# Cross attention of a decoder layer: row maxima packed on 128 partitions, another order of the steps, and expert weights scaled by ScalarE

## What is computed

```python
def _L0_xattn_ref(query, key, value, ...):          # query 32x112x256, key = value 32x375x256
    q, k, v = query @ qw.T + qb, key @ kw.T + kb, value @ vw.T + vb
    # 16 heads of 16; each head's q and k are cut in two halves of 8
    logits_1 = einsum('bhtd,bhsd->bhts', q1, k1) * SCALING
    logits_2 = einsum('bhtd,bhsd->bhts', q2, k2) * SCALING
    a1, a2 = softmax(logits_1), softmax(logits_2)
    diff_weights = a1 - lam * a2
    attn_output = einsum('bhts,bhsd->bhtd', diff_weights, v) * (1.0 - LAMBDA_INIT)
    return attn_output (heads joined) @ out_proj_weight.T + out_proj_bias
x = _layernorm(x + attn(x)); x = _layernorm(x + xattn(x, ctx, ctx)); x = _layernorm(x + ffn(x))
```

## Time and profile before

| | us |
|---|---|
| median of the runs (3 runs, 1745.75 to 1752.3) | 1746.22 |
| span of the profiled execution | 1765.9 |
| start of the first cross maxima to the last item's projection read | 438.8 to 1174 |
| cross turn without routing work | 21.06 |

### The profile page before, as it was taken

One profiled execution on the slowest core, in us unless ns is written; L12 is line 12 of the kernel. 1 busy time (PEld: TensorE's weight loads), 2 busy tenths in 40 slices (PEclk: granted clock), 3 DMA queues, 4 the chain that ended last, 5 costly groups with the idle time before them and its releaser, 6 DMA issues. The chain is left out here.

```text
span 1765.9 us, 46393 instructions
## 1 busy us (share of the span) xinstructions
PE 1566.4 (89%) x17664; PEld 1193.8 (68%) x17664; DVE 1117.6 (63%) x2617; ACT 897.4 (51%) x2175; POOL 759.0 (43%) x916
## 2 busy tenths in 40 slices
PE   4899999995899998999899989847999999999991
PEld 2577777774466666666566666526888888888891
DVE  5566666664788888878877877643454444444443
ACT  2345544543466666666666656523444444444444
POOL 6334334432675555776577567530111211212212
PEclk9899999998799999999999989868999999999996
DMA  6666666653665555565455445237777777767744
GB/s 179 181 182 185 190 190 187 185 154 77 161 170 150 143 141 138 148 160 144 136 157 158 136 116 162 72 125 274 250 247 245 256 241 246 268 228 252 273 139 176
DMA packets 205509, 318.93 MB, mean 181 GB/s; under 512 B 61000, under 2 KB 174056, under 8 KB 205288
## 3 DMA queue, kind: packets, MB, share of 16 engines
q1 hardware_dynamic: 180648, 248.48, 46.8%
q0 software_dynamic: 21504, 66.19, 12.5%
q10 hardware_dynamic: 3136, 1.30, 0.3%
HBM read 224.52 MB, written 91.03 MB: 179 GB/s over the span
## 5 line engine op out<-in xcount | busy, mean ns | idle before, releaser
L1208 DVE TENSOR_REDUCE cross_mx<-cross_bank_max 112x2 f32<-112x750 f32 x512 | 457.9, 932 | 123.7 <-PE cross_bank_max L1323 120.4
L1021 ACT ACTIVATE cross_probs<-cross_bank_score 125x448 f32<-125x448 f32 x768 | 399.0, 546 | 255.0 <-PE cross_bank_score L1313 220.1
L1323 PE MATMUL cross_bank_max<-ckst,cqst 96*112 96x375 f16 x1024 | 265.2, 342 | 31.1 <-DVE cross_mx L1208 20.4
L1500 POOL DMA_INDIRECT acc<-experts_y,experts_dest_i x64 | 98.7, 1543 | 442.7 <-ACT experts_y L1537 372.4
L1577 DVE TENSOR_TENSOR experts_hid<-experts_bank_h,experts_gated 128x256 f32<-128x256 f32 (+1 forms) x288 | 113.6, 394 | 261.6 <-ACT experts_gated L1526 257.7
L1313 PE MATMUL cross_bank_score<-cqst,ckst 97*125 97x448 f16 x768 | 267.8, 368 | 9.2 <-ACT cross_probs L1021 6.4
L1609 PE MATMUL experts_bank_h<-experts_x_hi,experts_w_more 128*128 128x256 f16 (+1 forms) x1536 | 234.0, 264 | 0.0
L1323 PEld LDWEIGHTS cross_bank_max<-ckst,cqst 96*112 96x112 f16 x1024 | 116.6, 133 | 125.0 <-DVE cross_mx L1208 99.3
L1609 PE MATMUL experts_bank_h<-experts_x_lo,experts_w_more 128*128 128x256 f16 (+1 forms) x768 | 196.2, 264 | 0.0
L1526 ACT ACTIVATE experts_gated<-experts_bank_h 128x256 f32<-128x256 f32 (+1 forms) x288 | 103.7, 360 | 166.9 <-PE experts_bank_h L1609 163.4
L1339 PE MATMUL cross_bank_out<-cross_probs,cross_val 125*32 125x112 f32 x6144 | 181.2, 266 | 1.5 <-issue 1.5
(11 more groups left out here) (241 smaller groups left out, 3045.9 us busy)
## 6 DMA issues: line engine op xcount, KB each, us to landing
experts_w_more<-w_halves SPq DMA_DIRECT2D x24, 3072.0 KB, 12.2
w<-w_halves SPq DMA_DIRECT2D x12, 3072.0 KB, 12.6
cross_ew<-in_experts POOLq DMA_DIRECT2D x32, 768.0 KB
w_halves<-cross_ew_half POOLq DMA_DIRECT2D x32, 768.0 KB, 7.5
ckst<-cross_k SPq DMA_DIRECT2D x96, 187.5 KB
cross_v<-front_v SPq DMA_DIRECT2D x24, 531.2 KB
cross_val<-cross_v SPq DMA_DIRECT2D x32, 398.4 KB
front_src<-in_ctx_t SPq DMA_DIRECT2D x24, 500.0 KB, 8.9
```

What stands on the lines that cost most here:

```text
L1021: nc.scalar.activation(probs[:, e % PROBS], bank_score[e % 2][0:SC, 0:4 * T], ACT.Exp, scale=CROSS_SCALE).then_inc(probs_ready, 1)
L1208: nc.vector.tensor_reduce(mx[:, b % nb, 2 * n:2 * n + 2], bank_max[n % 2][0:T, :, 0:S], AX.X, ALU.max).then_inc(max_read, 1)
L1323: last = nc.tensor.matmul(bank_max[n % 2][0:T, i, 0:S], qst[0:STACK, p, u // 4, (u % 4) * T:(u % 4 + 1) * T], kst[0:STACK, p, u // 4, :], ...
```

## The change

In `cross`:

- The query rows of an item are cut into 28 stripes of 128 rows (`stripe`) in place of 32 units of 112. Fourteen pairs take the place of sixteen, each reduced over 128 partitions. Where a stripe crosses from one group of 4 units (448 rows) to the next, which stripes 3, 10, 17 and 24 do, it is computed by two matmuls of 64 stationary columns each, into partitions 0 to 63 and 64 to 127. The row transposes and their DMAs go by 14 stripes of 128.
- `MAX_AT` and `REDUCE_AT` list the parts of the fourteen pairs in PE's and in DVE's stream. The order of the steps becomes `turn`, `score`, `row1`, `out1`, `heads`, `row0`, `proj`, `out0`, with other parts, and `turn`, `score`, `row1` and `row0` are read in the same part in which they are computed.
- The multiplication of the expert weights by 64 moves from POOL to ACT (`scale_weights`, after the exponentials of parts 13, 14 and 15). `ew` and `ew_half` and their semaphores are doubled, and loads run two cuts ahead.

```diff
-STEP_AT = {"turn": (1, -2), "row1": (4, 0), "score": (6, -2), "out1": (8, -1), "heads": (13, -1),
-           "row0": (15, 1), "proj": (17, -1), "out0": (21, 0)}
-READ_AT = {"turn": (2, -2), "row1": (5, 0), "score": (7, -2), "out1": (9, -1), "heads": (14, -1),
-           "row0": (16, 1), "proj": (18, -1), "out0": (22, 0)}
-EVACUATE_AT = ((14, 0), (2, -1))
-AGGREGATE_AT, NORMALISE_AT = 19, 23
+STEP_AT = {"turn": (2, -2), "score": (4, -2), "row1": (6, 0), "out1": (8, -1), "heads": (11, -1), "row0": (14, 1), "proj": (15, -1), "out0": (17, 0)}
+READ_AT = {"turn": (2, -2), "score": (4, -2), "row1": (6, 0), "out1": (9, -1), "heads": (12, -1), "row0": (14, 1), "proj": (17, -1), "out0": (20, 0)}
+EVACUATE_AT = ((15, 0), (4, -1))
+AGGREGATE_AT, NORMALISE_AT = (18, -1), (23, -1)
...
+SCALE_AT = (13, 14, 15)
...
-def maximum_at(e):
-
-    return SPAN // 3 * 2 * (e // SPAN) + e % SPAN - FIRST_MAX if e % SPAN >= FIRST_MAX else None
+QUERIES = UNITS * T
+LANES = 128
+STRIPES = QUERIES // LANES
+PAIRED = STRIPES // 2
+MAX_AT = (1, 3, 4, 6, 6, 10, 11, 14, 15, 17, 17, 20, 21, 23)
+REDUCE_AT = (0, 1, 1, 3, 7, 10, 12, 13, 17, 18, 19, 19, 20, 23)
+
+
+def at_part(table, e):
+
+    return [n for n, at in enumerate(table) if at == e]
+
+
+def stripe(j):
+
+    lo, hi, wide = LANES * j, LANES * (j + 1), 4 * T
+    cuts = sorted({lo, hi, *(g * wide for g in range(GROUPS) if lo < g * wide < hi)})
+    return [(a // wide, a % wide, a - lo, b - a) for a, b in zip(cuts, cuts[1:])]
...
-        mx = ph.sb("mx", [T, nb, UNITS], F32)
-        neg_mx = ph.sb("neg_mx", [16, nb, 2, T], F16)
+        mx = ph.sb("mx", [LANES, nb, STRIPES], F32)
+        neg_mx = ph.sb("neg_mx", [PAIRED, nb, 2, LANES], F16)
...
-        ew = ph.sb("ew", [128, CUT], F32)
+        ew = ph.sb("ew", [128, 2, CUT], F32)
         ew_big = ph.sb("ew_big", [128, CUT], F32)
-        ew_half = ph.sb("ew_half", [128, 2, CUT], F16)
+        ew_half = ph.sb("ew_half", [128, 2, 2, CUT], F16)
...
-                        wait(sp, ew_stored, 16 * CUTS)
+                        for p in range(2):
+                            wait(sp, ew_stored[p], 16 * CUTS // 2)
...
-                pool.dma_start(ew[:], a["experts"][0]).then_inc(ew_loaded, 16)
+                for b in range(2):
+                    pool.dma_start(ew[:, b], a["experts"][b]).then_inc(ew_loaded[b], 16)
...
                 def split_weights(b, group, ready):
-                    wait(pool, ew_loaded, 16 * (b + 1))
-                    wait(pool, ew_stored, 16 * b)
+                    p = b % 2
+                    wait(pool, ew_stored[p], 16 * (b // 2))
                     for i in range(pieces):
                         cols = slice(i * piece, (i + 1) * piece)
                         n = pieces * b + i + 1
-                        pool.tensor_scalar(ew_big[:, cols], ew[:, cols], WSCALE, None, ALU.mult).then_inc(ew_big_ready, 1)
                         wait(pool, ew_big_ready, n)
-                        if i == pieces - 1 and on(b + 1):
-                            pool.dma_start(ew[:], a["experts"][b + 1]).then_inc(ew_loaded, 16)
-                        pool.tensor_copy(ew_half[:, 0, cols], ew_big[:, cols]).then_inc(ew_hi_ready, 1)
+                        if i == pieces - 1 and on(b + 2):
+                            pool.dma_start(ew[:, p], a["experts"][b + 2]).then_inc(ew_loaded[p], 16)
+                        pool.tensor_copy(ew_half[:, p, 0, cols], ew_big[:, cols]).then_inc(ew_hi_ready, 1)
                         wait(pool, ew_hi_ready, n)
-                        pool.tensor_tensor(ew_half[:, 1, cols], ew_big[:, cols], ew_half[:, 0, cols],
+                        pool.tensor_tensor(ew_half[:, p, 1, cols], ew_big[:, cols], ew_half[:, p, 0, cols],
                                            ALU.subtract).then_inc(ew_ready, 1)
                         scatter(group, ready, i)
                     wait(pool, ew_ready, pieces * (b + 1))
-                    pool.dma_start(w_halves[b], ew_half[:]).then_inc(ew_stored, 16)
+                    pool.dma_start(w_halves[b], ew_half[:, p]).then_inc(ew_stored[p], 16)
...
-                        nc.scalar.activation(neg_mx[:, p, h], bank[0:16, 0:T], ACT.Copy, scale=-1.0).then_inc(read[name], 1)
+                        nc.scalar.activation(neg_mx[:, p, h], bank[0:PAIRED, 0:LANES], ACT.Copy, scale=-1.0).then_inc(read[name], 1)
                         wait(act, read[name], b + 1)
-                        act.dma_start(qst[STACK:STACK + 1, p, 4 * h:4 * h + 4, :].rearrange("o g (i t) -> o (g i) t", t=T),
-                                      neg_mx[:, p, h]).then_inc(row_loaded[h][p], 16)
+                        act.dma_start(qst[STACK:STACK + 1, p, 4 * h:4 * h + 4, :].rearrange("o g n -> o (g n)").rearrange(
+                            "o (j n) -> o j n", n=LANES), neg_mx[:, p, h]).then_inc(row_loaded[h][p], 16)
...
+                def scale_weights(b, i):
+                    cols = slice(i * piece, (i + 1) * piece)
+                    wait(act, ew_loaded[b % 2], 16 * (b // 2 + 1))
+                    wait(act, ew_ready, pieces * (b - 1) + i + 1)
+                    nc.scalar.activation(ew_big[:, cols], ew[:, b % 2, cols], ACT.Copy, scale=WSCALE).then_inc(ew_big_ready, 1)
...
+                        for i in at_part(SCALE_AT, e) if on(c + 2) else ():
+                            scale_weights(c + 2, i)
...
-                        if e == AGGREGATE_AT and on(c - 1):
-                            wait(dve, stats_ready, c)
                         if (c, e) in (LAMBDA_AT[0], LAMBDA_AT[2]):
                             difference(LAMBDA_AT.index((c, e)))
-                        n = maximum_at(e)
-                        if n is not None and on(c + lead):
+                        for n in at_part(REDUCE_AT, e) if on(c + lead) else ():
                             b = c + lead
-                            wait(dve, max_full, 2 * GROUPS * b + n + 1)
-                            nc.vector.tensor_reduce(mx[:, b % nb, 2 * n:2 * n + 2], bank_max[n % 2][0:T, :, 0:S],
+                            wait(dve, max_full, PAIRED * b + n + 1)
+                            nc.vector.tensor_reduce(mx[:, b % nb, 2 * n:2 * n + 2], bank_max[n % 2][:, :, 0:S],
                                                     AX.X, ALU.max).then_inc(max_read, 1)
-                        if e == AGGREGATE_AT and on(c - 1):
-                            p = (c - 1) % nb
+                        if e == AGGREGATE_AT[0] and on(c + AGGREGATE_AT[1]):
+                            b = c + AGGREGATE_AT[1]
+                            p = b % nb
+                            wait(dve, stats_ready, b + 1)
                             nc.vector.bn_aggr(mv[:, p], stats[:, p]).then_inc(mv_ready, 1)
...
-                    wait(pe, max_read, 2 * GROUPS * b + n - 1)
+                    wait(pe, max_read, PAIRED * b + n - 1)
                     for i in range(2):
-                        u = 2 * n + i
-                        last = nc.tensor.matmul(bank_max[n % 2][0:T, i, 0:S], qst[0:STACK, p, u // 4, (u % 4) * T:(u % 4 + 1) * T],
-                                                kst[0:STACK, p, u // 4, :], start=True, stop=True)
+                        for g, col, lane, size in stripe(2 * n + i):
+                            last = nc.tensor.matmul(bank_max[n % 2][lane:lane + size, i, 0:S], qst[0:STACK, p, g, col:col + size],
+                                                    kst[0:STACK, p, g, :], start=True, stop=True)
...
-                        wait(pe, max_read, 2 * GROUPS * b + GROUPS * (h + 1))
-                        last = nc.tensor.transpose(bank[0:16, 0:T], mx[:, p, 16 * h:16 * h + 16], ident[0:T, 0:T])
+                        wait(pe, max_read, PAIRED * b + PAIRED // 2 * (h + 1))
+                        last = nc.tensor.transpose(bank[0:PAIRED, 0:LANES], mx[:, p, PAIRED * h:PAIRED * (h + 1)], ident[:])
...
-                        n = maximum_at(e)
-                        if n is not None and on(c + lead):
+                        for n in at_part(REDUCE_AT, e) if on(c + lead) else ():
                             b = c + lead
-                            wait(dve, max_full, 2 * GROUPS * b + n + 1)
-                            nc.vector.tensor_reduce(mx[:, b % nb, 2 * n:2 * n + 2], bank_max[n % 2][0:T, :, 0:S],
+                            wait(dve, max_full, PAIRED * b + n + 1)
+                            nc.vector.tensor_reduce(mx[:, b % nb, 2 * n:2 * n + 2], bank_max[n % 2][:, :, 0:S],
                                                     AX.X, ALU.max).then_inc(max_read, 1)
-                        if e == AGGREGATE_AT and on(c - 1):
-                            p = (c - 1) % nb
+                        if e == AGGREGATE_AT[0] and on(c + AGGREGATE_AT[1]):
+                            b = c + AGGREGATE_AT[1]
+                            p = b % nb
+                            wait(dve, stats_ready, b + 1)
                             nc.vector.bn_aggr(mv[:, p], stats[:, p]).then_inc(mv_ready, 1)
```

(21 more changed lines are left out.)

1 line of the change is left out of this document (removed).

## The result

The changed kernel takes 1836.57 us (median of 4 runs, 1831.94 to 1843.27) where the kernel before takes 1746.89 us (median of 4). The ratio is 1.0516 with a 95% interval of 1.0487 to 1.0545: 5% slower. Forecast were 1716 us and a range of 1688 to 1742, so the sign was wrong too.

A forecast was written before the change was run, and what follows sets the result against it. No engine alone bounds it: PE and DVE hand bank pairs to and fro in the cross phase. Terms of -1.0 us a turn over 32 turns, +2 at the start, made -30 us: 1716 us, 8-in-10 range 1688 to 1742.

The forecast's parts named there:

- POOL's removed work: Cross phase: 4.5 of POOL's 12.82 us a turn go; POOL not on the path, so 0 gain.
- Rival C: Cross phase: `row1` DMA, issued a part later, lands late for part 12; slower, up to 1777 us; chance 0.10.
- -1.2 for DVE: Cross phase: two fewer reduces shrink PE's 1.6 us wait for DVE; -1.2 us a turn.
- +0.4 for the splits: Four split stripes: standstills around 64 column matmuls, as at the weighing, cost +0.4 us a turn.
- -0.5 and +0.3 for the steps: New step order, per turn: `row0`'s wait for ACT's read of `heads` goes, -0.5 us; `proj` waits, +0.3 us.
- -0.2 for the routing turns: Longer turns carrying DVE's routing operations: fewer reduces beside them give -0.2 us in the mean turn (0 to -0.5).
- ACT's operations: Weight scaling on ACT, three pieces a turn: 0.60 us each, with 0.2 us a turn reaching the path (0 to 0.8).
- The issue itself: ACT's DMA issues: two a turn at 0.5 us each, not counted as busy.
- The start: Before the first scores: ACT's read of the row maxima moves from 448.3 to about 451.9; +2 us taken.

The follow-up runs named there:

- e4_before_scale: The kernel before with only the weight scaling moved to ACT (parts 13 to 15) and loads and halves doubled; 1820.41 us, ratio 1.0442.
- e9_pool_hold: The changed kernel with the multiplication back on POOL, and POOL's load and store held until the turn's `row1` DMA has landed; 1710.32 us, ratio 0.9774.
- e8_stripes: The kernel before with the 14 pairs on 128 partitions and doubled weight buffers; steps, reads and POOL's multiplication as before; 1760.84 us, ratio 1.007.
- e10_no_split: e8_stripes with each of the four crossing stripes computed by one 128-column matmul, leaving out maxima of 64 rows; 1743.6 us, ratio 0.9969.
- e5_before_again: The kernel before, unchanged, run once more for a second profile; 1750.95 us, span 1749.2 us.
- e6_hold_next: The changed kernel plus the hold alone: POOL issues its load and store only after that turn's `row1` DMA has landed; 1734.03 us, ratio 0.9914.

## Why the prediction was wrong, point by point

**The step that failed** is the sentence on POOL's removed work, "POOL is not on the path in such a turn; 0". Its 4.5 us less were costed by who waits for POOL's results, which is nobody. They should have been costed by what POOL issues: its load and its store moved ahead of the DMA of `row1`, which was then 2.2 us late in nearly every turn, and nearly every such standstill was followed by a stretch at 1.2 GHz. Taken out by the hold alone, this is 102 us, 3.3 us a turn. With the order of before the same move of POOL's transfers gave a wait of 1.1 us (e4_before_scale); the other half I put down to the new order, in which the row leaves a part later. The issue times of both transfers were in the trace that I had.

**Rival C** named the right DMA, the right part and a slack of 3.5 us (in the instance above 638.5 - 634.76 = 3.7). It was priced with landings of at most 5.4, all taken while POOL's transfers stood elsewhere, at 1.9 us a turn, and got a chance of 0.10. Measured were 5.3 to 7.0 us from issue to score, median 6.2, a wait of 2.2 us and on top of it the clock, which no rival had. C's mechanism came true by a cause that C did not name.

**DVE and the order.** -1.2 for DVE, +0.4 for the splits, -0.5 and +0.3 for the steps, -0.2 for the routing turns make -1.2 for the mean turn. The kernel that has these parts, and the doubled buffers and the hold besides, is e9_pool_hold. Its mean turn is 20.28 for 21.58, -1.3 (undisturbed 19.9 for 21.1), and it is 39 us faster. The sum is right; whether each term is, or errors in them cancel, no run shows, since the steps were not tried by themselves. By e8_stripes and e10_no_split the pairs alone give next to nothing in the old parts, so the gain belongs to the pairs together with `MAX_AT`, `REDUCE_AT` and the new steps. Which of these it is was not tried.

**The split stripes.** +0.4 was forecast, from the weighing's standstills; measured +0.5 (e8_stripes against e10_no_split, in the order of before). The Trainium skill, page TensorEngine Tiling (Array Packing), section Key Properties, says that a change of tiling mode drains TensorE; the "issue" waits at the maxima, 42.7 us at the 64 column loads of the changed kernel, agree.

**ACT's operations.** 0.60 us each was forecast, 0.631 measured:

```profile
L1035 ACT ACTIVATE cross_ew_big<-cross_ew x96: 612/631/643, 444.1 to 1186.7; 128x512 f32<-128x512 f32 x96
```

The duration was right and the cover wrong: 0.2 a turn was forecast on the path, 0.9 is there in parts 13 to 15, and 0.3 in parts 7, 13 and 19. In parts 14 and 15 ACT also has the read of `row0` with its DMA issue and the evacuation, and no weighing beside them. The issue itself grew: put at 0.5 us, it held ACT's queue for 0.752 (median), where that of before took 0.511.

**The start.** ACT waits for POOL's subtractions as forecast and reads the row at 451.82 (forecast 451.9); the row leaves at 452.10, before at 448.57:

```profile
451.28 0.63 ACT L1035 ACTIVATE cross_ew_big<-cross_ew 128x512 f32<-128x512 f32 x1 [1.16 <-POOL cross_ew_half L971]
451.82 0.25 ACT L1016 ACTIVATE cross_neg_mx<-cross_bank_step 14x128 f16<-14x128 f32 x1
452.10 1.43 ACTq L1018 DMA_DIRECT2D cqst<-cross_neg_mx  x1
...
459.39 1.00 PE L1337 MATMUL cross_bank_score<-cqst,ckst 97*125 97x448 f16 x2 [9.81 <-DMA cqst<-cross_neg_mx]
```

The first score is 3.8 us later than in the first profile of before, and 5.8 later than in e5_before_again (453.58), from which the 7.6 us are counted; I had taken 2 of 0 to 3.5. The rest of the 7.6 is in the first turn. Most of the 7.6 goes with the hold: in e6_hold_next the first score starts at 456.80 and the first norm step only 2.1 us after that of e5_before_again.

**Left open:** which of POOL's two transfers does the harm, and whether SP's twelve loads, which run beside and behind them, are what the row in fact waits for. A hold of one transfer alone was not tried.

## What to carry to other kernels

When an engine that nobody waits for gets faster, list the transfers that it issues, and look at what else is in flight in the stretch to which they move; a DMA of a few KB on which TensorE waits needs its slack measured against its landing with those transfers ahead of it. The cheapest repair was to let the idle engine wait: 102 us for one semaphore wait in front of two bulk transfers. Where a stretch is to hide added work, look at the part of the order and not only at the engine's busy share: the same three operations cost 0.9 or 0.3 us a turn here.

## What the runs showed of the hardware that I had not expected

- A transfer of 3.5 KB started no packet for up to 4.3 us (median 3.5) with 1.5 MB of POOL's queue and SP's twelve loads in flight, where the same DMA of before, in the instance shown, had all packets started within 3 us.
- Standstills of PE of 2.2 us in the mean (2.56 in the instance shown), one in nearly every turn, went with stretches of mostly 3.4 us at 1.2 GHz, for a mean clock of 0.92.
- A reduce on 128 partitions takes what one on 112 takes (931 and 932 ns); a seventh more rows cost nothing there:

```profile
L1229 DVE TENSOR_REDUCE cross_mx<-cross_bank_max 128x2 f32<-128x750 f32 x448 | 402.4, 931 | 216.5 <-PE cross_bank_max L1347 214.8
```
